# A two-layer fused kernel: order of the first loads, weight halves on VectorE, paired transposing loads

## What is computed

```python
x = L0_attn_x
x = x + 0.5 * _L0_ffn_ref(_layernorm(x), ...)     # 16 experts, 4 per token, and a shared expert
x = x + _L0_attn_ref(_layernorm(x), ...)
x = x + 0.5 * _L0_ffn_ref(_layernorm(x), ...)
x = x + 0.5 * _L1_ffn_ref(_layernorm(x), ...)     # 32 experts of 96, all computed, times their factor
x = x + _L1_attn_ref(_layernorm(x), ...)          # state-space block
x = x + 0.5 * _L1_ffn_ref(_layernorm(x), ...)
```

## Time and profile before

| | |
|---|---|
| median of three runs | 994.18 us |
| profiled execution | 983.99 us |
| its span on the core | 982.2 us |
| mean granted clock of TensorE | 0.959 |
| busy in the span: TensorE, VectorE, ScalarE, GpSimd | 855.6, 712.4, 500.0, 477.3 us |

### The profile page before, as it was taken

One profiled execution on the slowest core, in us unless ns is written; L12 is line 12 of the kernel. 1 busy time (PEld: TensorE's weight loads), 2 busy tenths in 40 slices (PEclk: granted clock), 3 DMA queues, 4 the chain that ended last, 5 costly groups with the idle time before them and its releaser, 6 DMA issues.

```text
span 982.2 us, 20723 instructions
## 1 busy us (share of the span) xinstructions
PE 855.6 (87%) x6872; PEld 557.1 (57%) x6872; DVE 712.4 (73%) x1392; ACT 500.0 (51%) x929; POOL 477.3 (49%) x464
## 2 busy tenths in 40 slices
PE   2767788999748899788889897899999899999997
PEld 1356666777424667647675554454566445665564
DVE  6897326988778888736447987888978777785554
ACT  2867553688515677536767852345333543333332
POOL 3865278424667344288825866532443224432322
PEclk9979999999559999999999998999999999999999
DMA  8796546632122224847965522111110211112221
GB/s 303 287 219 154 138 146 123 135 85 59 60 65 78 64 55 102 254 153 154 195 166 167 166 100 68 47 54 47 51 57 23 76 51 47 54 41 92 73 68 65
DMA packets 123267, 106.62 MB, mean 109 GB/s; under 512 B 75672, under 2 KB 97944, under 8 KB 123168
## 3 DMA queue, kind: packets, MB, share of 16 engines
q1 hardware_dynamic: 117024, 88.51, 32.1%
q0 software_dynamic: 6144, 16.79, 6.0%
HBM read 58.98 MB, written 30.02 MB: 91 GB/s over the span
## 4 chain that ended last, share of the span: by engine, by line
PE 60%; issue 7%; DVE 6%; POOL 3%; ACT 2%; DMA 2%; SPq 1%; POOLq 0%; DVEq 0%; ACTq 0%
PE ps L1063 24%; PE ps L1110 12%; PE ps L1038 7%; PE ps L1092 5%; PE ps L1254 2%; PE ps L1078 1%; PE ps L1177 1%; PE ps L1216 1%; PE ps L1211 1%; PE ps L1285 1%; DVE hid L1330 1%; DVE hid L1324 1%; POOL back L760 1%; PE ps L1274 1%; POOL xs_dram L745 1%
## 5 line engine op out<-in xcount | busy, mean ns | idle before, releaser
L717 POOL TENSOR_TENSOR hh<-hid,hh 128x512 f16<-128x512 f32 x120 | 143.5, 1198 | 238.7 <-ACT hh L829 238.4
L1324 DVE SCALAR_TENSOR_TENSOR hid<-gtanh,ps 128x512 f32<-128x512 f32 (+2 forms) x184 | 114.4, 622 | 160.4 <-ACT gtanh L808 145.8
L1063 PE MATMUL ps<-xhi,whi 128*128 128x512 f16 x480 | 186.8, 389 | 24.4 <-DVE hid L1324 20.1
L808 ACT ACTIVATE gtanh<-ps 128x512 f32<-128x512 f32 (+2 forms) x184 | 100.4, 545 | 204.7 <-PE ps L1063 169.3
L1063 PE MATMUL ps<-xlo,whi 128*128 128x512 f16 x480 | 186.5, 388 | 0.0
L1063 PE MATMUL ps<-xhi,wlo 128*128 128x512 f16 x480 | 186.1, 388 | 0.0
L1110 PE MATMUL ps<-whi,hh 128*128 128x256 f16 x960 | 174.5, 273 | 5.2 <-POOL hh L717 5.2
L1038 PE MATMUL ps<-whi,xs_sb 128*128 x992 | 130.5, 245 | 34.1 <-issue 23.6
L1338 DVE SCALAR_TENSOR_TENSOR hid<-hid,ps 128x512 f32<-128x512 f32 (+2 forms) x184 | 114.6, 623 | 28.9 <-PE ps L1038 12.2
L1110 PE MATMUL ps<-wlo,hh 128*128 128x256 f16 x480 | 131.0, 273 | 0.0
L829 ACT ACTIVATE hh<-hid 128x512 f16<-128x512 f32 x120 | 75.1, 626 | 95.1 <-DVE hid L1330 64.8
(11 more groups left out here) (208 smaller groups left out, 1587.4 us busy)
## 6 DMA issues: line engine op xcount, KB each, us to landing
ys_dram<-y_sb SPq DMA_DIRECT2D x60, 256.0 KB, 2.5
xs_sb<-c_dram SPq DMA_DIRECT2D x64, 192.0 KB, 2.7
scr<-w_in SPq DMA_DIRECT2D x28, 384.0 KB, 4.9
scr<-we_in SPq DMA_DIRECT2D x32, 304.0 KB, 4.6
xs_sb<-c_dram SPq DMA_DIRECT2D x64, 128.0 KB, 2.9
xs_sb<-c_dram SPq DMA_DIRECT2D x64, 64.0 KB, 2.7
xs_dram<-y_sb SPq DMA_DIRECT2D x1, 3968.0 KB, 15.0
scr<-ws_in SPq DMA_DIRECT2D x8, 384.0 KB, 7.1
```

The costliest lines, as they stand in the source:

```text
L717: pool.tensor_tensor(hlo[:, k, :], hid[:, k % 2, :], hhi[:, k, :], ALU.subtract).then_inc(lo_done, 1)
L808: act.activation(gtanh[:, n % 2, 0:w], ps[:, G_BANK, 0:w], ACT.Tanh, scale=0.5 / W_SCALE)\
L1063: mm = pe.matmul(ps[:, bank, :], w[:, off:off + P], a[:, kc, t0:t0 + HN], start=(i == 0), stop=(i == 3 * KC - 1))
L1324: dve.scalar_tensor_tensor(out=hid[:, k, 0:w], in0=gtanh[:, k, 0:w], scalar=1.0, in1=ps[:, G_BANK, 0:w], op0=ALU.add, op1=ALU.mult).then_i ...
```

## The change

The first loads are reordered: the constants are issued by ScalarE's queue, the second half of x comes after the six shared pieces, and the clearing after two routed pieces. All 40 pieces of the first layer and all 28 dense ones get their low half on VectorE, from the unscaled piece; the scaling on ScalarE and the subtraction on GpSimd are gone for them. A routed unit's two blocks are loaded by one transposing DMA of 256 rows. The high half of a dense piece 8 or later waits for the routed units whose experts lie under it instead of the whole pass. The order strings of all engines are new. VectorE's new order has the low halves of pieces 9 to 19 between the fourth and the fifth shared unit, those of 20 to 37 by the seventh routed unit, dense pieces 0 to 12 within the last routed pass, 13 to 20 in the first six dense units, and 21 to 27 behind the nineteenth. GpSimd's has two sends (of four DMAs each) on either side of one low half. SP's has 32 weight pieces ahead of the first routed load. In the last part of the diff, the strings are cut to the beginning of three.

```diff
     for g in range(NW0):
+        if g == NSH:
+            put("SP", "w", "load_x1", 0)
         put("SP", "w", "load_w0", g)
         put("ACT", "w", "w0_hi", g)
-        if g < NSH or g % 2 == 0:
+        if g < NW0:
             put("DVE", "w", "w0_lo", g)
...
         if g == NSH + 1:
-            put("SP", "b", "blank", 0)
+            put("SP", "w", "blank", 0)
...
         put("ACT", "w", "w1_hi", j)
-        put("ACT", "w", "w1_scale", j)
-        put("POOL", "w", "w1_lo", j)
+        put("DVE", "w", "w1_lo", j)
...
-        xs_sb = sb("xs_sb", [P, 2 * XRING, 2 * KC, P], F16)
+        xs_sb = sb("xs_sb", [P, XRING, 2 * KC, 2 * P], F16)
...
         def piece_on_dve(g):
 
-            return g < NSH or g % 2 == 0
+            return True
...
+        def chunk_free(n):
+
+            last = ((n + 1) * CW - 1 - EXP0) // EW
+            return (HN // P) * (last + 1) // 2
...
-            sp_.dma_start(const[:, 0:P], const_in[:, 0:P]).then_inc(consts_loaded, 16)
-            sp_.dma_start(const[:, P:P + NBLK], const_in[:, 2 * P:2 * P + NBLK]).then_inc(consts_loaded, 16)
-            sp_.dma_start(tri, const_in[:, P:2 * P]).then_inc(consts_loaded, 16)
-            sp_.dma_start(rw[:, :], rw_in).then_inc(consts_loaded, 16)
-
-            sp_.dma_start(x[:, HT:TILES, :], xv[:, HT:TILES, :]).then_inc(x_half1, 16)
...
+                elif name == "load_x1":
+                    sp_.dma_start(x[:, HT:TILES, :], xv[:, HT:TILES, :]).then_inc(x_half1, 16)
...
-                    for j in range(xs_loads(b)):
-                        rows = slice((2 * b + j) * P, (2 * b + j + 1) * P)
-                        sp_.dma_start_transpose(xs_sb[:, 2 * k + j, :, :], xs_dram[rows, :])\
-                            .then_inc(xs_loaded[k], 16)
+                    w = xs_loads(b)
+                    rows = slice(2 * b * P, (2 * b + w) * P)
+                    sp_.dma_start_transpose(xs_sb[:, k, :, 0:w * P], xs_dram[rows, :]).then_inc(xs_loaded[k], 16)
...
         def _(act):
+            act.dma_start(const[:, 0:P], const_in[:, 0:P]).then_inc(consts_loaded, 16)
+            act.dma_start(const[:, P:P + NBLK], const_in[:, 2 * P:2 * P + NBLK]).then_inc(consts_loaded, 16)
+            act.dma_start(tri, const_in[:, P:2 * P]).then_inc(consts_loaded, 16)
+            act.dma_start(rw[:, :], rw_in).then_inc(consts_loaded, 16)
             act.wait_ge(consts_loaded, 64)
...
-                    if n == EXP0 // CW:
-                        act.wait_ge(down_done, UNIT[7] + NRT)
+                    if n >= EXP0 // CW:
+                        act.wait_ge(down_done, UNIT[7] + min(NRT, chunk_free(n)))
...
-                                mm = pe.matmul(ps[:, bank, j * I0:(j + 1) * I0], xs_sb[:, slot + j, a + kc, :],
+                                mm = pe.matmul(ps[:, bank, j * I0:(j + 1) * I0], xs_sb[:, slot, a + kc, j * P:j * P + P],
...
+                elif name == "w1_lo":
+                    g = NW0 + n
+                    dve.wait_ge(w_hi, g + 1)
+                    dve.scalar_tensor_tensor(out=wlo[:, n * CW:(n + 1) * CW], in0=stage[:, g % SLOTS, :], scalar=W_SCALE,
+                                             in1=whi[:, n * CW:(n + 1) * CW], op0=ALU.mult, op1=ALU.subtract)\
+                        .then_inc(w_lo_dve, 1)
...
     "DVE":
-        "A2 B A C B D2 C A r2 B r w4 m2 w2 m2 w3 m2 w r B m2 C w2 m2 w r m2 C w2 r m2 r m2 r a w m2 r m w2 m2 w "
+        "A2 B w B C D C D w r m r m r w2 m w m r m w m w2 r w A m A m w11 m2 w B m2 w2 m2 B w m w m w m a m w2 m "
...
     "POOL":
-        "A4 x2 l x l2 w x w l w3 l w l w3 l w2 l w2 l w l w l w l3 w l5 x l x l x l2 x l2 c2 l c l c l c l A c l "
+        "A2 l x2 l x2 l2 A l A l14 x l x l2 x l x l c l c l c l c l2 c A c l c2 l3 A l4 P2 l P l P l P2 l P4 l P "
...
     "SP":
-        "b w23 l w3 l w4 l w2 l w2 l w l w l w4 y w l y l y l y l y2 l y l y l y l2 y7 l7 y2 l2 y3 l2 y l y l y "
+        "w34 l3 w2 l w2 l w2 l w2 y l w y l2 y2 l y l2 y2 l2 y2 l2 y7 l6 y l2 y2 l y2 l2 y l y l2 y2 l2 y7 l6 y "
```

More of the change, by code:

```diff
@@ L552, in xs_count @@
         def xs_count(r, b):
-            return sum(xs_loads(c) for p in RT_PASSES if p < r for c in range(b % XRING, NRT, XRING)) \
-                + sum(xs_loads(c) for c in range(b % XRING, b + 1, XRING))
+            return sum(ring_count(b % XRING, XRING, NRT) for p in RT_PASSES if p < r) + b // XRING + 1
         def xs_loads(c):
@@ L1006, in wait_shared @@
             def wait_shared(j):
-                pe.wait_ge(w_lo_dve, lo_count(j))
+                pe.wait_ge(*w_split(j))
             def wait_expert(e):
-                pe.wait_ge(w_lo_dve, lo_count(NSH + 2 * e))
-                pe.wait_ge(w_lo_pool, lo_count(NSH + 2 * e + 1))
+                pe.wait_ge(*w_split(NSH + 2 * e))
+                pe.wait_ge(*w_split(NSH + 2 * e + 1))
             def piece(name, n):
@@ L1167, in piece @@
                     pe.wait_ge(x_lo, ln_pair(ATTN_STAGE, n // 4, n // 2 % 2))
-                    pe.wait_ge(w_lo_dve, lo_count(NW0 - 2))
-                    pe.wait_ge(w_lo_pool, lo_count(NW0 - 1))
+                    pe.wait_ge(*w_split(NW0 - 2))
+                    pe.wait_ge(*w_split(NW0 - 1))
                     if n:
```

35 lines of the change are left out of this document (12 added, 23 removed), and 92 rows, old and new, of the table ORDER.

## The result

The kernel after takes 949.46 us in the median of four runs (948.83 to 952.12), beside 993.52 us for the kernel before on the same chip: ratio 0.9563, 95% interval 0.9530 to 0.9595. That is 44 us less, where I had forecast 20 and a range down to 36 less. The profiled execution took 948.97 us.

What follows compares the result with a forecast made beforehand. TensorE bounds the kernel, busy 855.6 of 982.2 us; gains come only from its 126.6 idle us and half-clock stretches. Terms 8 + 10 + 1 + 1 = 20 off the median 994.2 give 974 us, range 958 to 989.

Steps and rivals of the forecast that it cites:

- Start: Opening: reordered first loads bring the first routed gate to 58.8 us, 3.8 earlier; opening and first routed pass gain 8 us.
- I take 10: First dense pass: gain of 10 us, between nothing and 15.4 idle plus 2 for the clock.
- If half of the excess goes ...: First dense pass: with half the excess gone and added pieces waiting 0.5 us each, VectorE goes from 93.8 to 105.
- my measure of the excess: First dense pass: VectorE's time above undisturbed on 22 products and one addition, 22 us in 110.
- One transposing load per pair ... I take 1: Routed passes: 124 loads become 64, at 2.2 us of SP each; 1 us gained over four passes.
- the stretch from 250 hangs on the attention's end, which moves along with it: Attention's handover, 250 to 330 us: it does not cover up the 8 us gained earlier; no gain of its own.
- The one term that I had for order: Third dense pass, route and order: a gap there may shrink, 1 us.
- B: Opening: sends run late beside VectorE's pieces, routed pass starts at 65, total 982 us; chance 0.19.
- E: 28 to 75 and 500 to 560 us: VectorE becomes the bound, slower by 11, 1005 us; chance 0.08.
- F: Attention's handover: the gains are given back there, nothing measurable, 994 us; chance 0.04.
- D: More comes: one price per load instruction, shorter half clock in 250 to 330, both upper bounds; 959 us, chance 0.09.
- C: A stall lasts one instruction: 4 us in the opening, 3 in the dense pass; 987 us, chance 0.08.

Runs made afterwards that it cites:

- e13: The kernel before, unchanged, run again with a profile on the same chip as e14: 983.67 us, ratio 1.0007.
- e14: The kernel after, unchanged, run on the same chip as e13: 942.10 us, ratio 0.9599 to the kernel before.
- e12: The kernel after with ScalarE scaling each dense piece again and VectorE subtracting: 955.28 us, ratio 0.9635 to the kernel before.
- e18: The kernel after with the old order of 22 units around the attention's handover, conversions and loads kept: 957.71 us, ratio 0.9753 to the kernel before.
- e16: The kernel after with extra GpSimd instructions behind low halves in the last dense pass: 943.19 us, one execution.
- e17: The kernel after with three extra 384-column GpSimd instructions behind low halves of units 4 to 19, last dense pass: 939.60 us, one execution.
- e5: The kernel after, unchanged, run again beside the kernel before on the same chip: 950.45 us, ratio 0.9552.
- e15: The kernel after with the clearing behind two shared pieces instead of eight pieces: 947.46 us, ratio 0.9645 to the kernel before.

## Why the prediction was wrong in size

The sign and the opening were right, and so was the mechanism of the dense pass in the kernel before: GpSimd's conversions hold VectorE, and gates wait behind that (e13). The total was half of what came, and the steps that failed are the sizes of three terms, one of them put at nothing.

- **Start**: as predicted in its times. Clearing landed at 26.8 (28 forecast), the last send ended at 50.3 (52), first routed gate 58.87 (58.8), no VectorE instruction over 3 us ahead of 60. In part the gate's time is luck: I had the shared pass end before 58 with nothing waiting for it, and it ended with the gate, held by a low half behind the sends. With the first routed pass this part was to give 8 us; e13 and e14 show 10.9.
- **"I take 10"** for the first dense pass, between 0 and 17.4, failed: it gave 20.9, above my upper bound. The step is "If half of the excess goes ...": TensorE's idle time in this pass fell from 15.2 us (e13) to 0.8 (e14), so 14.4 of it went and not about half. The clock gave more than I had as well: 101.8 us of busy TensorE became 96.3, 5.6 us where I had 2. And ScalarE's scaling ahead of its tanh, which I put at nothing, costs 5 us when it comes back (e12). The factor's product kept 0.91 us in the mean, above the near 0.8 that I named, and TensorE was idle for 0.6 us all the same, so my measure of the excess was not what a gate waited for.
- **"One transposing load per pair ... I take 1"** failed: 10.5 us undone and 3 alone. The SyncE price that I took (2.2 us) was wrong, it is the lower bound, 1.23. The larger error was to size it by the sentence that TensorE waits for rows once: I asked who waits for the rows, and not who stands behind their issues. In the first routed pass the weight pieces do.
- **The order**: "the stretch from 250 hangs on the attention's end, which moves along with it" failed. My sum has nothing for the handover, and 9.8 us more were gained up to the third shared pass. I took the rewritten lists as neutral. e18 shows that the old order of 22 units brings the whole pause back (43.7 us) and costs 15.6 us in all. The one term that I had for order, 1 us in the third dense pass, was right: the gap ahead of that pass went from 7.2 us (e13) to 6.1 (e14).
- **The base**: the profile that I read was of a sort of chip on which the kernel before is 10 us faster than in the runs shown. The change is worth 40.5 us there, 43.5 on the other. This accounts for 3 us, no more.
- **The rivals**: B (late sends) didn't come: 1.05 us each beside VectorE's conversions. E didn't come: VectorE is busy for 86 of 96 us, and nothing waits. F is the opposite of what the handover did. D had the right direction, with the paired load's single price among its reasons, and stopped at 35. C's time didn't come either; its rule of one instruction is discussed next. The Trainium skill's sentence (SBUF — State Buffer, "Who interferes with whom") that "Whoever issues first gets the shared pair for the whole instruction" stands there in the point on VectorE's two-port modes; carried over to two SBUF inputs, as I did, it fits e16 and e17, in which VectorE waits for one instruction and then gets in, and 87 of 125 cases. It does not fit the 32 cases in which VectorE began first, was then held, and was held over the whole train; these took 2.8 to 9.6 us each.

The parts don't add: undone one at a time they cost 24 (dense), 10.5 (paired load), 10 (clearing) and 16 (order), in sum 60 for a change worth 41 to 44, while two of them alone gave 8 and 3. It would fit that an order written out by hand for a set of parts makes each part look dear when it is taken out, and cheap when it is put alone into the order of another set. This is not shown: no run put a part into the kernel before together with a new order, and what each is worth by itself stays open.

## What to carry to other kernels

Price an issue on a shared DMA queue by everything that stands behind it, not by who waits for its data, and a conversion by every queue that it sits in (here SyncE for the loads, ScalarE for the scaling, GpSimd for the low half). Where a change rewrites a written-out order, read the new order around each handover of the old profile before calling it neutral. And take the profile and the timed runs from one chip before making a sum in single microseconds.

## What the hardware showed that I had not expected

- Chips differ by about 1.1% for the same kernel: medians of 982.5, 982.6 and 983.1 us on three chips, 992.6, 993.5 and 994.0 us in the other groups, with no overlap (978.9 to 987.0 and 989.0 to 996.0). The granted clock in the records differs little and does not sort them well (means of 0.967, 0.966 and 0.963 on the three, 0.961 and 0.962 at 994.0 and 992.6). The kernel after is spread less, 942.1 to 950.5, and all of it lies in the first 288 us (e5, e14). Why is open.
- A VectorE instruction with two SBUF inputs that is already under way when a train of two-input GpSimd instructions begins either gets through (35 of 67) or waits for the whole train (32 of 32 held ones, up to 9.6 us for 0.79 us of work); one that begins inside the train and is held mostly waits for one instruction (87 of 99). No run shows why; the held ones began 0.03 to 0.4 us ahead of the train, and so did many of those that got through.
- A transposing load of 256 rows costs SyncE's queue 1.23 us, one of 128 rows 1.27 (medians): one price per instruction at these two sizes.
- The issue right behind the clearing of 3968 KB holds SyncE's queue until about 5 us before the clearing lands: 10.2 us in e15, 9.4 in the kernel before, 13.1 in the kernel after, where it is a piece that is needed late.
